# Reading the accumulator banks out in another order in the query, key and value stage of a two-layer attention block

## Chip, cores and metric

One core of one Trainium2 chip runs the whole program in one launch. The metric is the device time of one execution in microseconds (us); the kernel before is given by the median of three runs. All points in time below are microseconds from the start of the profiled execution's span.

## The reference, cut to what matters

Two layers run one after the other on four batches of 512 tokens with 512 features. The change sits at the entry of the second layer's self-attention:

```python
x = rms_norm(hidden_states, ln_in_w)
mixed = jnp.where(vm, x @ v_qkv, x @ l_qkv)
q, k, v = jnp.split(mixed, 3, axis=-1)
q, k, v = (heads(q, NH, HD), heads(k, NH, HD), heads(v, NH, HD))
q, k = apply_rotary(q, k, position_ids, l)
```

`vm` marks the tokens that take the second expert's weights (`v_qkv`); all others take the first's (`l_qkv`). The norm's factor is one number per token, so the kernel multiplies it in behind the products: into the rotary tables for queries and keys, and as a column of factors for the values.

## The kernel before, in words

The stage is the function `queries_values_keys` (from line 687). Each product is made in three matmuls of rounded and rest parts (`three`, lines 103 to 107), so every weight and every token tile is split into a rounded tile and a rest. A batch has three projections of eight steps each: queries, values, keys (in the last batch queries, keys, values). The first four steps of a projection use the first expert, the other four the second; if the flag of early tokens is not set, the second half is narrowed to the last 128 tokens. TensorE reads that flag and branches behind the fourth query step of every batch. The three projections alternate between two groups of four accumulator banks, so a projection starts when the group has been read out.

The order on each engine is written out by hand, and the engines meet only at semaphores:

- TensorE (lines 1074 to 1128): `project` makes one step, `sums` multiplies the summed squares with a matrix of ones (line 1101; two products, the plain norm and the weighted one, into the first two banks of the values' group), and in the fifth value step four small products turn the norm factors into a column (line 1117).
- ScalarE (lines 807 to 906): `round_x` and `round_w` round token and weight tiles (819, 811), `square` squares the stream (829), `keep_plain` copies queries or keys out of the banks (839), `round_piece` rounds a finished piece (846), `root` makes a reciprocal square root by Ln and Exp (859, 861), and `keep_values` reads the values out with the column of factors (871). `root(i, 0)` reads the first sums from their bank; `root(i, 1)` reads what VectorE made of the second.
- VectorE: `mask_x` and `rest_x` prepare tokens (979, 986), `rest_w` makes a weight's rest (967), `second_sums` squares the first root and multiplies it with the second sums out of their bank (994, 997), `tables` makes the factors and the scaled cosine and sine (1003 to 1006), `turn_pieces` does the rotary part of four pieces (1017 to 1027), and then the column is copied out of its bank (1053, tile `rs_col`).
- GpSimd: `add_squares` (919) and `scale_pieces` (930), the cosine products.
- SP issues all loads and stores of the stage: weights (91), the next batch's stream (772), two stores for each finished piece (753, 755) and one for each value tile (792). In the last batch it also loads self-attention's first keys before the last four pieces' stores, and at the end a row of ones (795).

The semaphore `s_tab` counts the five VectorE instructions of the tables; the values' group of banks is free when its second one (the read of the second sums) has run. Weights of the keys are steps 16 to 23: in the first batch ScalarE rounds them behind the copies of the queries, and VectorE makes their rests before it turns the first piece.

Of the kernel before, what the change touches and what calls it, by code (L numbers as in the profile page):

```python
# [7 lines left out]
P = 128  # L8
# [16 lines left out]
def program(nc, t, out):  # L25
# [21 lines left out]
    with ExitStack() as keep:  # L47
# [639 lines left out]
        def queries_values_keys(more_h, more_l, k_r, q_r, v_r, s_key, s_value, s_first):  # L687

            names = ("s_tt s_k s_ku0 s_ku1 s_eu s_hin s_x s_xh s_xl s_sq s_sum s_ss s_rs s_tab s_r0u s_pl s_sf s_t1 s_t2 s_rp s_rh s_rl "
# [13 lines left out]
            with ctx:  # L703
# [27 lines left out]
                with nc.Block() as block:  # L731
                    @block.sync
                    def _(sp):
# [28 lines left out]
                        for i in range(B):  # L762
# [15 lines left out]
                            if i == B - 1:  # L778
# [9 lines left out]
                                for j in range(DT):  # L788
                                    store_piece(2 * DT * i + DT + j)
                            for a in range(ST):  # L790
# [3 lines left out]
                        sp.wait_ge(s["s_wu"], NT * B)  # L794
                        sp.dma_start(k_r[3 * HD:3 * HD + 1, :, :].bitcast(f32).rearrange("a (r h) n -> a r (h n)", r=8),
                                     ones_d[:, 0:SELF_RING * 4 // 8 * S].rearrange("(a r) n -> a r n", a=1)).then_inc(s_first, 16)
# [10 lines left out]
                    def _(act):  # L807
# [40 lines left out]
                        def root(i, n):  # L848
# [10 lines left out]
                            nc.scalar.activation(rs[:, :], src, ACT.Ln, bias=eps_col[:, 0:1], scale=1.0 / D).then_inc(s["s_rs"], 1)  # L859
                            act.wait_ge(s["s_rs"], 4 * i + 2 * n + 1)  # L860
                            nc.scalar.activation(rs[:, :], rs[:, :], ACT.Exp, scale=-0.5).then_inc(s["s_rs"], 1)

                        def keep_values(i):
# [3 lines left out]
                            for a in range(ST):  # L867
                                o = ST * i + a
                                if o >= 2 and not (i == B - 1 and a >= 2):
# [3 lines left out]
                                    .then_inc(s["s_vn"], 1)  # L873

# [7 lines left out]
                        for i in range(B):  # L882
# [9 lines left out]
                            keep_plain(i, 0)  # L892
                            if i == 0:
                                for n in range(2 * G, 3 * G):
                                    round_w(n)
                            for j in range(DT):
# [12 lines left out]
                    def _(pool):  # L909
                        def add_squares(i):  # L910

                            for n in range(2):
                                for k in range(1, DT):
# [3 lines left out]
                                    elif i:  # L917
                                        pool.wait_ge(s["s_ss"], 2 * (i - 1) + n + 1)
                                    nc.gpsimd.tensor_tensor(out=sq[:, 2 + n, :], in0=sq[:, 0 if k == 1 else 2 + n, :], in1=sq[:, k % 2, :],
# [23 lines left out]
                    def _(dve):  # L943
# [45 lines left out]
                        def second_sums(i):  # L989
# [5 lines left out]
                            dve.wait_ge(s["s_ss"], 2 * i + 2)  # L995
                            dve.wait_ge(s["s_tab"], 5 * i + 1)
                            nc.vector.tensor_tensor(out=rs1[:, :], in0=rs1[:, :], in1=ps[:, bank(3 * i + 1, 1), :], op=ALU.mult)\
# [9 lines left out]

                        def turn_pieces(i, group):

                            dve.wait_ge(s["s_tab"], 5 * (i + 1))  # L1010
                            for j in range(DT + 1):
                                o = 2 * DT * i + DT * group + j
                                if j < DT:
# [25 lines left out]
                        for i in range(B):  # L1039
# [10 lines left out]
                            dve.wait_ge(s["s_rc"], i + 1)  # L1050
                            if i:
# [1553 lines left out]
```

## Time and profile before

| | us |
|---|---|
| median of three runs | 2175.74 |
| lowest and highest run | 2171.53, 2179.38 |
| the profiled execution | 2180.68 |
| its span | 2178.7 |
| the stage of the change, in the span | 354.2 to 615.4 |

The profiled execution has a trace of every engine. A timeline row gives the start, the length and the instruction, and in brackets how long its engine stood idle before it and what ended that. Rows of the same line that follow one another are merged (x4), and their lengths may overlap. PE is TensorE, DVE is VectorE, ACT is ScalarE, POOL is GpSimd, SPq is SP's queue of transfers. Of matmuls the starts are recorded and the ends are modelled.

### The profile page before, as it was taken

To read this page: it belongs to the slowest core of one execution; us is meant where nothing else is said; L and a number is where in the kernel's file an instruction comes from. 1 tells how busy PE (TensorE), PEld (TensorE's weight loads), DVE (VectorE), ACT (ScalarE), POOL (GpSimd) and SP (SyncE) were. 2 spreads that over 40 slices of the span, in tenths; PEclk is the share of its full clock that TensorE was granted. 3 is DMA by queue.
4 is the path that set the end of the run, shared out by engine and by line. 5 is a ranking of instruction groups with operands and counts; after the bars stand their busy time and mean duration, and the time that the engine had idled before them with its cause. 6 is when DMAs were issued, how large, how long until landed. Compare 5 with 4: busy or idle time off the path is not lost. (4 is left out here: it accounts for less than half of the span.)

```text
span 2178.7 us, 32799 instructions
## 1 busy us (share of the span) xinstructions
PE 1996.9 (92%) x12654; PEld 1340.6 (62%) x12654; DVE 1523.9 (70%) x2111; ACT 1007.2 (46%) x1748; POOL 509.4 (23%) x496
## 2 busy tenths in 40 slices
PE   6999997799979997788879999999998799999997
PEld 5788875677845554676634444444434677878885
DVE  5676776588847775656579999999952565766563
ACT  1232314455425554444348888888884222221111
POOL 0321231133401222332201312223222212221211
PEclk9999998799969999999979999999999899999998
DMA  3222112333377663685545344354401333334332
GB/s 139 71 99 80 35 57 78 121 122 122 101 189 175 169 151 103 205 254 201 154 114 96 68 89 87 73 98 78 91 14 40 112 92 99 102 109 114 94 97 56
DMA packets 174793, 236.92 MB, mean 109 GB/s; under 512 B 26218, under 2 KB 103022, under 8 KB 172426
## 3 DMA queue, kind: packets, MB, share of 16 engines
q1 hardware_dynamic: 166480, 223.65, 38.3%
q0 software_dynamic: 7856, 10.90, 1.8%
q8 instruction: 112, 1.84, 0.4%
q14 instruction: 57, 0.47, 0.1%
q10 hardware_dynamic: 288, 0.08, 0.0%
HBM read 169.54 MB, written 62.91 MB: 107 GB/s over the span
## 5 line engine op out<-in xcount | busy, mean ns | idle before, releaser
L2120 ACT ACTIVATE pT_x<-ps 128x512 f32<-128x512 f32 (+1 forms) x832 | 451.3, 595 | 84.6 <-PE ps L2218 57.0
L2159 DVE TENSOR_REDUCE quarters<-ps 128x2 f32<-128x804 f32 x480 | 454.1, 992 | 45.5 <-PE ps L2190 44.7
L2233 PE MATMUL ps<-pT_x,vx_ring 128*17 128x256 f32 (+1 forms) x3328 | 261.5, 387 | 0.2 <-ACT osb_x L2102 0.2
L105 PE MATMUL ps<-mi_h,w_hi 128*128 128x512 f32 (+1 forms) x440 | 174.0, 395 | 12.8 <-DVE mi_l L2414 12.8
L2379 POOL TENSOR_TENSOR sg<-sg,keep_all 128x512 f32<-128x512 f32 (+1 forms) x55 | 88.1, 1602 | 386.0 <-ACT sg L2358 386.0
L106 PE MATMUL ps<-mi_h,w_lo 128*128 128x512 f32 (+1 forms) x440 | 173.2, 394 | 0.0
L107 PE MATMUL ps<-mi_l,w_hi 128*128 128x512 f32 (+1 forms) x440 | 173.1, 393 | 0.0
L1307 DVE TENSOR_REDUCE row_max_s<-ps 128x1 f32<-128x384 f32 (+3 forms) x176 | 109.4, 633 | 68.6 <-PE ps L1339 67.8
L1279 ACT ACTIVATE pT_s<-ps 128x512 f32<-128x512 f32 (+1 forms) x176 | 96.0, 558 | 117.6 <-PE ps L1364 115.6
L99 DVE CAST w_hi<-w_raw 128x512 fp32r<-128x512 f32 (+1 forms) x165 | 84.3, 511 | 72.4 <-PE ps L107 65.4
L2233 PEld LDWEIGHTS ps<-pT_x,vx_ring 128*17 128x17 f32 (+1 forms) x3328 | 55.6, 95 | 110.7 <-issue 68.8
L101 DVE TENSOR_TENSOR w_lo<-w_raw,w_hi 128x512 fp32r<-128x512 f32 (+1 forms) x165 | 114.8, 696 | 5.7
L2362 ACT ACTIVATE hid_h<-prod 128x512 fp32r<-128x512 f32 (+1 forms) x55 | 34.8, 634 | 177.4 <-DVE prod L2442 177.4
L2358 ACT ACTIVATE sg<-ps 128x512 f32<-128x512 f32 (+1 forms) x55 | 32.8, 596 | 164.7 <-PE ps L107 164.7
L289 ACT ACTIVATE pT<-ps 128x512 f32<-128x512 f32 (+1 forms) x52 | 31.0, 598 | 158.2 <-PE ps L107 158.2
L105 PEld LDWEIGHTS ps<-mi_h,w_hi 128*128 128x128 f32 (+1 forms) x440 | 82.3, 187 | 33.0 <-issue 13.6
L107 PEld LDWEIGHTS ps<-mi_l,w_hi 128*128 128x128 f32 (+1 forms) x440 | 82.2, 187 | 20.0
L106 PEld LDWEIGHTS ps<-mi_h,w_lo 128*128 128x128 f32 (+1 forms) x440 | 82.3, 187 | 19.1
L2442 DVE TENSOR_TENSOR prod<-ps,sg 128x512 f32<-128x512 f32 (+1 forms) x55 | 37.9, 689 | 80.1 <-PE ps L107 71.3
L105 PE MATMUL ps<-hid_h,w_hi 128*128 128x512 f32 (+1 forms) x220 | 87.9, 400 | 3.0 <-DVE hid_l L2446 3.0
L1339 PE MATMUL ps<-qkv_h,qkv_l 96*128 96x128 f32 (+3 forms) x256 | 90.5, 414 | 0.0
L329 POOL TENSOR_TENSOR sin_t<-sin_t,pT 128x512 f32<-128x512 f32 (+1 forms) x48 | 72.4, 1509 | 65.0 <-ACT pT L289 64.4
(350 smaller groups left out, 4821.0 us busy)
## 6 DMA issues: line engine op xcount, KB each, us to landing
qkv_l<-self_q_by_part SPq DMA_DIRECT2D x48, 256.0 KB, 4.4
qkv_h<-self_k_by_part SPq DMA_DIRECT2D x48, 256.0 KB, 6.7
w_raw<-L_xattn_l_gate SPq DMA_DIRECT2D x40, 256.0 KB, 2.9
w_raw<-L_xattn_l_up SPq DMA_DIRECT2D x40, 256.0 KB, 2.9
w_raw<-L_xattn_l_down SPq DMA_DIRECT2D x40, 256.0 KB, 2.7
kx_first<-cross_k_by_part SPq DMA_DIRECT2D x36, 200.2 KB, 7.2
cross_v_by_group<-v_aug SPq DMA_DIRECT2D x16, 442.0 KB, 3.9
vx_ring<-cross_v_by_group SPq DMA_DIRECT2D x16, 442.0 KB, 10.1
```

Of the source, the lines that this page charges most:

```text
L99: nc.vector.tensor_copy(hi, raw).then_inc(s_high, 1)
L101: nc.vector.tensor_tensor(out=lo, in0=raw, in1=hi.bitcast(f32), op=ALU.subtract).then_inc(s_split, 1)
L105: nc.tensor.matmul(dst, ah, bh, start=start, stop=False, **how)
L106: nc.tensor.matmul(dst, al, bh, start=False, stop=False, **how)
L107: return nc.tensor.matmul(dst, ah, bl, start=False, stop=stop, **how)
L1279: nc.scalar.activation(pT[:, u % 3, j:j + n, 0:width], heads_of(ps[:, SCORES + v % 3, :], n, width), ACT.Exp, scale=SCALE).then_inc(s["s_e ...
L1307: nc.vector.tensor_reduce(out=row_max[:, g % 2, j:j + heads, q], in_=heads_of(bank, heads, (q + 1) * P), axis=AX.X, op=ALU.max)\
L1339: last = nc.tensor.matmul(bank[:, m * width:(m + 1) * width], q_r[0:STACK, at + m, cut], k_r[0:STACK, at + m, 0:width], start=False, stop= ...
L2120: nc.scalar.activation(pT[0:kn, u % 3, j, :], ps[0:kn, 5 + v % 3, :], ACT.Exp, scale=SCALE)\
L2159: nc.vector.tensor_reduce(out=quarters[:, g % 2, pair, :, q, quarter], in_=ps[:, at:at + 2, 0:MAXW], axis=AX.X, op=ALU.max)\
L2233: last = nc.tensor.matmul(ps[j * HD:j * HD + CHD + 1, 4, queries], v_r[0:kn, g % RING, kt, j, :], pT[0:kn, u % 3, j, queries], start=kt == ...
L2379: nc.gpsimd.tensor_tensor(out=by_batch(sg[0:cn, c % 2, :]), in0=by_batch(sg[0:cn, c % 2, :]), in1=keep_all[0:cn, experts[i], :, rows(i)], ...
```

## The change

- The second sums are copied by ScalarE from their bank into the fourth tile of `sq`, between the Ln and the Exp of the first root; VectorE multiplies with that tile. The values' first product waits for this copy (`s_cp`) instead of VectorE's product. GpSimd's next use of the tile waits for VectorE's.
- The column of norm factors is copied before the fourth query piece instead of behind it; in the last batch before the third key piece.
- In the first batch the key weights are rounded before the queries are copied out, and the sums are multiplied behind the sixth query step, so behind the branch, instead of the fourth.
- In the last batch ScalarE issues the four value stores itself, and the row of ones is issued before the last key piece's stores.

```diff
--- before.py
+++ after.py
@@ -686,7 +686,7 @@
 
         def queries_values_keys(more_h, more_l, k_r, q_r, v_r, s_key, s_value, s_first):
 
-            names = ("s_tt s_k s_ku0 s_ku1 s_eu s_hin s_x s_xh s_xl s_sq s_sum s_ss s_rs s_tab s_r0u s_pl s_sf s_t1 s_t2 s_rp s_rh s_rl "
+            names = ("s_tt s_k s_ku0 s_ku1 s_eu s_hin s_x s_xh s_xl s_sq s_sum s_ss s_rs s_tab s_r0u s_cp s_pl s_sf s_t1 s_t2 s_rp s_rh s_rl "
                      "s_uh0 s_uh1 s_ul0 s_ul1 s_ul2 s_rc s_rcc s_vn s_uv0 s_uv1 s_hup " + WSEMS)
             ctx, sems = stage(names)
             s = dict(zip(names.split(), sems))
@@ -785,15 +785,16 @@
                                 self_key_loads(sp, 0, k_r, q_r, s_key)
                                 self_value_load(sp, 0, v_r, s_value)
                                 sp.dma_start(early_d.rearrange("b o n -> o (b n)"), early_v[:, :]).then_inc(s["s_eu"], 16)
-                                for j in range(DT):
+                                for j in range(DT - 1):
                                     store_piece(2 * DT * i + DT + j)
-                            for a in range(ST):
+                                sp.wait_ge(s["s_wu"], NT * B)
+                                sp.dma_start(k_r[3 * HD:3 * HD + 1, :, :].bitcast(f32).rearrange("a (r h) n -> a r (h n)", r=8),
+                                             ones_d[:, 0:SELF_RING * 4 // 8 * S].rearrange("(a r) n -> a r n", a=1)).then_inc(s_first, 16)
+                                store_piece(2 * DT * i + 2 * DT - 1)
+                            for a in range(ST if i < B - 1 else 0):
                                 sp.wait_ge(s["s_vn"], ST * i + a + 1)
                                 sp.dma_start(vs_d[turns[i]].rearrange("g p a n -> p a g n")[:, a, :, :],
                                              value_tile(i, a).rearrange("p (g n) -> p g n", n=P)).then_inc(s_uv[a % 2], 16)
-                        sp.wait_ge(s["s_wu"], NT * B)
-                        sp.dma_start(k_r[3 * HD:3 * HD + 1, :, :].bitcast(f32).rearrange("a (r h) n -> a r (h n)", r=8),
-                                     ones_d[:, 0:SELF_RING * 4 // 8 * S].rearrange("(a r) n -> a r n", a=1)).then_inc(s_first, 16)
                         sp.wait_ge(s["s_eu"], 16)
                         sp.wait_ge(s["s_r0u"], 16 * B)
                         for m in range(2):
@@ -857,6 +858,9 @@
                             else:
                                 act.wait_ge(s["s_tab"], 5 * i + 2)
                             nc.scalar.activation(rs[:, :], src, ACT.Ln, bias=eps_col[:, 0:1], scale=1.0 / D).then_inc(s["s_rs"], 1)
+                            if n == 0:
+                                act.wait_ge(s["s_ss"], 2 * i + 2)
+                                nc.scalar.activation(sq[:, 3, :], ps[:, bank(3 * i + 1, 1), :], ACT.Copy).then_inc(s["s_cp"], 1)
                             act.wait_ge(s["s_rs"], 4 * i + 2 * n + 1)
                             nc.scalar.activation(rs[:, :], rs[:, :], ACT.Exp, scale=-0.5).then_inc(s["s_rs"], 1)
 
@@ -871,6 +875,10 @@
                                 nc.scalar.activation(value_tile(i, a), ps[:, bank(3 * i + place(i, 1), a), :], ACT.Copy,
                                                      scale=rs_col[:, a:a + 1])\
                                     .then_inc(s["s_vn"], 1)
+                                if i == B - 1:
+                                    act.wait_ge(s["s_vn"], o + 1)
+                                    act.dma_start(vs_d[turns[i]].rearrange("g p a n -> p a g n")[:, a, :, :],
+                                                  value_tile(i, a).rearrange("p (g n) -> p g n", n=P)).then_inc(s_uv[a % 2], 16)
 
                         for n in range(2 * DT):
                             round_x(0, n)
@@ -889,10 +897,10 @@
                                 for j in range(2, DT):
                                     round_piece(2 * DT * (i - 1) + DT + j)
                             root(i, 1)
-                            keep_plain(i, 0)
                             if i == 0:
                                 for n in range(2 * G, 3 * G):
                                     round_w(n)
+                            keep_plain(i, 0)
                             for j in range(DT):
                                 round_piece(2 * DT * i + j)
                             if i == B - 1:
@@ -916,6 +924,8 @@
                                         pool.wait_ge(s["s_sum"], 3 * (2 * i + n) + k - 1)
                                     elif i:
                                         pool.wait_ge(s["s_ss"], 2 * (i - 1) + n + 1)
+                                        if n:
+                                            pool.wait_ge(s["s_tab"], 5 * (i - 1) + 2)
                                     nc.gpsimd.tensor_tensor(out=sq[:, 2 + n, :], in0=sq[:, 0 if k == 1 else 2 + n, :], in1=sq[:, k % 2, :],
                                                             op=ALU.add).then_inc(s["s_sum"], 1)
 
@@ -992,9 +1002,9 @@
                             if i:
                                 dve.wait_ge(s["s_rc"], i)
                             nc.vector.tensor_tensor(out=rs1[:, :], in0=rs0[:, :], in1=rs0[:, :], op=ALU.mult).then_inc(s["s_tab"], 1)
-                            dve.wait_ge(s["s_ss"], 2 * i + 2)
+                            dve.wait_ge(s["s_cp"], i + 1)
                             dve.wait_ge(s["s_tab"], 5 * i + 1)
-                            nc.vector.tensor_tensor(out=rs1[:, :], in0=rs1[:, :], in1=ps[:, bank(3 * i + 1, 1), :], op=ALU.mult)\
+                            nc.vector.tensor_tensor(out=rs1[:, :], in0=rs1[:, :], in1=sq[:, 3, :], op=ALU.mult)\
                                 .then_inc(s["s_tab"], 1)
 
                         def tables(i):
@@ -1005,11 +1015,20 @@
                             nc.vector.tensor_tensor(out=cos_r[:, :], in0=cos_t[:, :], in1=rs1[:, :], op=ALU.mult).then_inc(s["s_tab"], 1)
                             nc.vector.tensor_tensor(out=sin_r[:, :], in0=sin_t[:, :], in1=rs1[:, :], op=ALU.mult).then_inc(s["s_tab"], 1)
 
+                        def keep_columns(i):
+
+                            dve.wait_ge(s["s_rc"], i + 1)
+                            if i:
+                                dve.wait_ge(s["s_vn"], ST * i)
+                            nc.vector.tensor_copy(rs_col[:, :], ps[:, bank(3 * i + place(i, 1) - 1, 0), 0:ST]).then_inc(s["s_rcc"], 1)
+
                         def turn_pieces(i, group):
 
                             dve.wait_ge(s["s_tab"], 5 * (i + 1))
                             for j in range(DT + 1):
                                 o = 2 * DT * i + DT * group + j
+                                if (j, group) == ((DT - 1, 0) if i < B - 1 else (2, 1)):
+                                    keep_columns(i)
                                 if j < DT:
                                     dve.wait_ge(s["s_pl"], o + 1)
                                     if o:
@@ -1047,10 +1066,6 @@
                             turn_pieces(i, 0)
                             if i == B - 1:
                                 turn_pieces(i, 1)
-                            dve.wait_ge(s["s_rc"], i + 1)
-                            if i:
-                                dve.wait_ge(s["s_vn"], ST * i)
-                            nc.vector.tensor_copy(rs_col[:, :], ps[:, bank(3 * i + place(i, 1) - 1, 0), 0:ST]).then_inc(s["s_rcc"], 1)
                             if i + 1 < B:
                                 find_keep(i + 1)
                                 for n in range(2 * DT + 1):
@@ -1074,7 +1089,7 @@
                                     if i:
                                         pe.wait_ge(s["s_vn"], ST * i)
                                 elif place(i, part) == 1:
-                                    pe.wait_ge(s["s_tab"], 5 * i + 2)
+                                    pe.wait_ge(s["s_cp"], i + 1)
                                     if i:
                                         pe.wait_ge(s["s_pl"], 2 * DT * i)
                                 else:
@@ -1107,7 +1122,7 @@
                             for m in steps:
                                 n = G * parts[m // G] + m % G
                                 project(i, n, t0)
-                                if m == 3:
+                                if m == (3 if i else 5):
                                     sums(i, 0)
                                     sums(i, 1)
                                 if n == G + 4:
```

## Rows read from the trace of the kernel before

**Rows 1.** Busy time in a stretch (TensorE matmul, TensorE load, VectorE, ScalarE, GpSimd), then granted clock.

```profile
423.40:479.70 56.30, 52.97 (x264) 43.94 (x265) 46.05 (x69) 28.76 (x45) 21.53 (x14) 0.94 0.34 118
```

**Rows 2.** Waits of TensorE, 345 to 625 us: us in total, times, longest.

```profile
PE ps L105 <- DVE rs_col L1053: 10.0, 3, 7.4
...
PE ps L105 <- DVE rs L997: 6.8, 3, 2.8
PE ps L1101 <- POOL sq L919: 6.3, 2, 4.0
...
PE ps L105 <- issue: 3.8, 1, 3.8
```

**Rows 3.** Timeline of TensorE, first batch: start, us, instruction, idle before it.

```profile
381.92 2.08 PE L1101 MATMUL ps<-sq,ones 128*128 128x512 f32 x2 [3.97 <-POOL sq L919]
387.75 0.45 PE L105 MATMUL ps<-xe1h,qkv_h 128*128 128x128 f32 x1 [3.76 <-issue]
```

**Rows 4.** Timeline of ScalarE, first batch.

```profile
382.52 1.28 ACT L861 ACT_TABLE_LOAD   x1
383.82 0.63 ACT L861 ACTIVATE rs<-rs 128x512 f32<-128x512 f32 x1
...
399.51 2.06 ACT L839 ACTIVATE plain<-ps 128x512 f32<-128x512 f32 x4 [10.84 <-PE ps L107]
...
410.02 0.64 ACT L811 ACTIVATE qkv_h<-w_raw 128x512 fp32r<-128x512 f32 x1 [0.95 <-DMA w_raw<-L_xattn_v_qkv]
```

**Rows 5.** Timeline of VectorE, first batch.

```profile
390.03 0.68 DVE L1006 TENSOR_TENSOR sin_r<-sin_t,rs 128x512 f32<-128x512 f32 x1
402.12 4.11 DVE L967 TENSOR_TENSOR qkv_l<-w_raw,qkv_h 128x512 fp32r<-128x512 f32 x4 [11.40 <-ACT qkv_h L811]
...
411.31 0.74 DVE L1017 STREAM_SHUFFLE swapped<-plain 128x512 f32<-128x512 f32 x1
```

**Rows 6.** Timeline of GpSimd, first and second batch.

```profile
400.25 4.23 POOL L930 TENSOR_TENSOR t<-plain,cos_r 128x512 f32<-128x512 f32 x3 [18.38 <-ACT plain L839]
...
465.94 4.70 POOL L930 TENSOR_TENSOR t<-plain,cos_r 128x512 f32<-128x512 f32 x3 [8.96 <-DVE sin_r L1006]
```

**Rows 7.** Timeline of SP's queue, value stores of the first and second batch.

```profile
424.08 1.00 SPq L792 DMA_DIRECT2D self_v_by_group<-v_nat  x2
...
480.38 5.82 SPq L792 DMA_DIRECT2D self_v_by_group<-v_nat  x4
```

**Rows 8.** Timeline of VectorE, second batch: first and fourth query piece, norm columns.

```profile
465.90 0.74 DVE L1017 STREAM_SHUFFLE swapped<-plain 128x512 f32<-128x512 f32 x1
...
475.55 0.76 DVE L1017 STREAM_SHUFFLE swapped<-plain 128x512 f32<-128x512 f32 x1
...
479.43 0.16 DVE L1053 COPY rs_col<-ps 128x4 f32<-128x4 f32 x1
```

**Rows 9.** Timeline of ScalarE, second batch: a token rounding, the third key piece.

```profile
433.54 0.63 ACT L819 ACTIVATE xe0h<-full_x 128x512 fp32r<-128x512 f32 x1 [1.57 <-PE ps L107]
...
456.98 0.61 ACT L846 ACTIVATE rows_h<-t 128x512 fp32r<-128x512 f32 x1
```

**Rows 10.** Timeline of VectorE, second batch: rests of the last two key pieces.

```profile
458.25 1.47 DVE L1027 TENSOR_TENSOR t<-t,rows_h 128x512 fp32r<-128x512 f32 x2
```

**Rows 11.** Timeline of VectorE, last batch: third key piece.

```profile
598.30 0.74 DVE L1017 STREAM_SHUFFLE swapped<-plain 128x512 f32<-128x512 f32 x1
```

**Rows 12.** Timeline of TensorE, norm columns of the second and the last batch.

```profile
474.49 1.05 PE L1117 MATMUL ps<-ones,rs 1*128 1x1 f32 x8
...
602.55 1.05 PE L1117 MATMUL ps<-ones,rs 1*128 1x1 f32 x8
```

**Rows 13.** Timeline of ScalarE, last batch: last key piece.

```profile
605.81 0.63 ACT L846 ACTIVATE rows_h<-t 128x512 fp32r<-128x512 f32 x1 [2.11 <-DVE t L1023]
```

**Rows 14.** Tile ident: ScalarE's issue, ns min/median/max.

```profile
L263 ACTq DMA_DIRECT2D ident<-c_ident x1: 426/426/426, 0.7 to 0.7; - x1
```

**Rows 15.** Timeline of SP's queue, last batch: last value stores.

```profile
609.19 1.49 SPq L792 DMA_DIRECT2D self_v_by_group<-full_x  x2
```

## Prediction

> **What bounds the kernel now.** The change touches one stage, from 354.2 to 615.4 us of the span, so I read that stage and left the page's totals. First the busy times from one start of the key projection to the next [rows 1]: TensorE is busy 52.97 of 56.3 us, VectorE 46.05. That alone would make TensorE the limit. Then who keeps TensorE waiting [rows 2]: the norm-column copy (rs_col, 10.0 us in three waits, the longest 7.4, in the first batch), the second-sum product (rs, 6.8 in three), GpSimd's sums of squares (6.3, both in the first batch), and one gap of 3.8 that no other engine explains. The first two end on the read-out side. So a ring sets the period: ScalarE reads the values out, rounds the next batch's tokens and reads the keys out; VectorE turns the key pieces, makes the tables, turns the query pieces, and its norm-column copy lets the values be read. TensorE's idle time counts only where it delays a link of this ring.
>
> I work against the profiled execution, 2180.68 us (span 2178.7 and 2.0 around it); the median of the three runs is 4.9 us lower, and I take the gain in us off that median. A measurement of this kernel can tell about 0.3%, here 6.5 us.
>
> **First batch: the only large term.** Now TensorE finishes its fourth query step, waits for GpSimd's second sum, multiplies it from 381.92 to 384.00, and stands 3.76 us before the next product [rows 3]; that gap holds the branch on the early flag. After the change two more steps lie in front of the sums, so the branch comes while products are still queued. Every batch has this branch, and the list of waits has a gap of this size once [rows 2]. I take it as covered; if the cover fails it costs up to 3.8 (a rival). GpSimd's sum is not moved, so the second sum product still ends at 384.0 (between 381.9, the wait alone, and 387.8 with the gap).
>
> On ScalarE the first root's Exp ends at 383.82 + 0.63 = 384.45 [rows 4]. The new Copy waits in front of that Exp for the second product: 384.0 + 0.6 (four plain copies take 2.06, about 0.5 each, plus a hand-over), then the Exp's table load, 1.28 [rows 4], then Exp 0.63: 386.6, so 2.15 later. What follows, up to the sine table, keeps its instructions: 390.03 + 0.68 = 390.71 becomes 392.9 [rows 5]. Bounds of a Copy between Ln and Exp: 0 if it slips into waiting time, one more table load (1.28) if it needs its own; the trace has Copy only behind Exp, without a load, so I take none.
>
> Key weights: now VectorE's first split of them starts at 402.12, because ScalarE rounds them behind four copies that wait for the queries, at 399.51 [rows 4, 5]. Between 390.71 and 402.12 VectorE has nothing to do. With the rounding first, the first split follows the sine table at 392.9. From first split to first turned piece the trace takes 411.31 - 402.12 = 9.2 [rows 5]: SP reloads four weight buffers as splits free them, and the last rounding, held by its load, ends at 410.02 + 0.64, that is 8.5 after the first split [rows 4]. The same 9.2 gives 402.1. The price is that the query copies stand behind the last rounding: from 392.9 + 8.5 = 401.4 instead of 399.5, just ahead of VectorE. **So the first turn starts 9.2 us earlier.** If the loads are no faster than half of this, 4.6.
>
> This turn then loses a cover. Today GpSimd's three cosine products run from 400.25, before VectorE begins; in the next batch they start together with it at 465.94 [rows 6]. From first turned piece to first value store it is 424.08 - 411.31 = 12.8 in the first batch and 480.38 - 465.90 = 14.5 in the second [rows 5, 7, 8]. The first batch now behaves as the second: store at 402.1 + 14.5 = 416.6, **7.5 us earlier**; at best, without that stretch, 9.2.
>
> **Norm columns between pieces.** The copy is issued before the fourth piece, in the second batch 475.55 instead of 479.43 [rows 8]. TensorE's keys can start some 4 us sooner. But ScalarE cannot: its fourth rounding still comes first, and SP issues the value stores behind the fourth piece's store, so the first store moves by 0.3 at most, and 0.2 go to the copy itself. I count nothing. What TensorE gives back: in the first token loop ScalarE waits twice for products, 1.57 in the row shown [rows 9]. Such waits go; VectorE is nearly gapless beside them, so I take **0.5** once (0 to 3.1).
>
> **Second sums by ScalarE.** TensorE's values no longer wait for VectorE's product: 6.8 us of TensorE idle [rows 2] go, but off the ring; TensorE then waits for the norm columns instead. The Copy costs ScalarE 0.5 per batch. Behind it stands the third key piece's rounding, 456.98 + 0.61 = 457.6, whose reader on VectorE starts at 458.25 [rows 9, 10]: 0.65 slack, so 0; uncovered it is at most 0.5 x 3 = 1.5.
>
> VectorE's product now reads two SBUF tiles, like the sine multiply (0.68, alone) [rows 5]. At that point GpSimd stands idle until the sine table exists, 8.96 us in the second batch [rows 6]; I add nothing. The Trainium skill (GPSIMD Engine Reference, section 1, Specifications) says the two engines contend for SBUF when a VectorE instruction has two SBUF inputs, which speaks against the move out of PSUM. By that rule alone the 1.7 us stretch above would be the scale of the loss, some 1.7 per batch, where both engines work; here they don't.
>
> **Last batch and tail.** ScalarE stands some 0.2 before the last key copies, for TensorE; that goes, **0.2**. Norm columns before the third key piece: VectorE now reaches that piece at 598.30, and TensorE's columns end at 602.55 + 1.05 = 603.6 [rows 11, 12]. TensorE gains on the ring twice: its keys one batch before start 479.43 - 475.55 = 3.9 sooner [rows 8], and up to 2.8 more go with the wait on rs. So with the ring at -8.2 the columns end near 603.6 - 8.2 - 6.7 = 588.7, against an arrival at 598.3 - 8.2 + 0.2 = 590.3: no wait. The values then follow ScalarE's last rounding (605.81 + 0.63 = 606.4) [rows 13] and no longer for the columns. But ScalarE now issues each store itself: four reads of about 0.65 with the hand-over, and between them three issues of 0.43 (ScalarE's only kind of issue in the trace) to 0.75 (SP's for these tiles) [rows 14, 15], give 3.9 to 4.85 from last rounding to last issue; now the last of SP's two goes at about 609.9, 3.5 behind it. **Loss 0.9** (0.4 to 1.4). The row of ones, moved on SP past the last key piece's store, costs that store one issue; it still lands before the values. In the first batches SP's order is unchanged.
>
> Sum: -7.5 - 0.5 - 0.2 + 0.9 = **-7.3 us**; 2175.74 - 7.3 = **2168.4**. The next stage begins behind a barrier and all of it follows, so the gain passes through.
>
> **Rivals.**
> 1. *The branch gap stays.* The gap of rows 3 follows the branch into the first-batch sums: the ring starts up to 3.8 later, gain 3.5, 2172.2. For: the gap is there with nothing else that the profile names. Against: the other batches show none. The Trainium skill (Runtime: NRT & Kernel Launch, section Instruction fetch mechanics) says that a taken branch breaks the sequential prefetch and stalls; no run here shows whether queued products cover it in this batch. Chance 0.17.
> 2. *The weights come no sooner.* ScalarE's rounding stands on the loads and the query copies stand behind it, so half of the 9.2 goes: -2.7, 2173.0. Chance 0.10.
> 3. *TensorE is the bound after all.* Then all its waits but the first and the seam go: 10.0 + 6.8 + 6.3 + 3.8 = 26.9 [rows 2, 3], 2148.8. For: 94% busy. Against: each of those waits ends on the ring. Chance 0.07.
> 4. *Slower: VectorE blocks on the norm columns.* With its copy between pieces, VectorE stands still if the columns come after it. Today they end at 475.54 when it arrives at 475.55, and in the last batch 5.3 after it [rows 8, 11, 12]. If TensorE's columns fall x behind the ring in the last three batches, the loss is 3x + 5.3; from x = 2.8 it eats the gain and 0.3% more; at 3 it is 14.3 - 7.3 = +7.0, 2182.7. For: the margin today is nil. Against: the wait in front of the values is what the change shortens. Chance 0.06.
>
> **Numbers.** Forecast 0.60. Its own bounds: best, the sums 2.1 sooner and the stretch of 1.7 away, -11.1; worst, an extra table load, the Copy uncovered, the dearer issues and nothing for the token loop, -3.5. About three quarters of it lie beyond 6.5: 0.45, with rival 3 faster 0.52. Same: 0.15 + 0.17 + 0.10 = 0.42. Slower 0.06. The range of 2163.5 to 2174.0 takes in the forecast's bounds and rivals 1 and 2 with a little of the scatter of the three runs; 3 and 4 stay outside.
>
> **What would show it.** Right: first turned piece near 402, its Exp near 386.6, first value store near 416.6, no TensorE wait on rs, but waits on rs_col of some 4 to 5 us left in three batches, periods of the store still 55 to 56, self-attention's first product near 608. Wrong: the gap before the second query half still 3.8 with the sums behind it (rival 1), weight roundings that end after 404 (2), a period near 50 (3), VectorE idle before rs_col (4).

## Result and profile after

The median after is 2161.45 us (2159.43 to 2162.76, five runs) against 2175.74 before: ratio 0.9926, interval 0.9908 to 0.9943. The kernel is 14.3 us faster where 7.3 were forecast, 2 us below the low end of the range. The span fell from 2178.7 to 2159.6; 5.2 of these 19.1 lie behind the stage, where nothing was changed, and the profiled execution before was 4.9 above its median. I therefore measure the stage in the traces: from the first masked token tile to the first product of self-attention it took 258.28 before and 244.85 after, **13.4 us less**.

TensorE's waits from 345 to 625 us, kernel after (us, times, longest), answer to [rows 2]:

```profile
PE ps L105 <- DVE rs_col L1023: 11.4, 3, 4.7
...
PE ps L106 <- issue: 2.5, 1, 2.5
...
PE ps L1116 <- POOL sq L929: 0.8, 1, 0.8
```

The wait on rs is gone and the norm columns have three of 3 to 5 us, much as forecast. The gap behind the branch is still 2.5 us long, but now it lies ahead of the sums (timeline of TensorE, against [rows 3]):

```profile
376.85 0.22 PE L106 MATMUL ps<-xe1h,qkv_l 128*128 128x128 f32 x1 [2.52 <-issue]
...
381.48 2.07 PE L1116 MATMUL ps<-sq,ones 128*128 128x512 f32 x2 [0.81 <-POOL sq L929]
```

ScalarE, first batch (against [rows 4]): Copy, table load, Exp, then the roundings ahead of the query copies.

```profile
383.59 0.60 ACT L863 ACTIVATE sq<-ps 128x512 f32<-128x512 f32 x1 [1.53 <-PE ps L1116]
384.20 1.28 ACT L865 ACT_TABLE_LOAD   x1
385.50 0.63 ACT L865 ACTIVATE rs<-rs 128x512 f32<-128x512 f32 x1
...
398.48 1.28 ACT L812 ACTIVATE qkv_h<-w_raw 128x512 fp32r<-128x512 f32 x2 [1.46 <-DMA w_raw<-L_xattn_v_qkv]
399.66 2.04 ACT L840 ACTIVATE plain<-ps 128x512 f32<-128x512 f32 x4
```

VectorE (against [rows 5]): the first four splits take 2.49 us instead of 4.11, and the first turned piece starts at 400.40 instead of 411.31.

```profile
392.32 2.49 DVE L977 TENSOR_TENSOR qkv_l<-w_raw,qkv_h 128x512 fp32r<-128x512 f32 x4
...
400.40 0.75 DVE L1036 STREAM_SHUFFLE swapped<-plain 128x512 f32<-128x512 f32 x1
...
409.70 0.16 DVE L1023 COPY rs_col<-ps 128x4 f32<-128x4 f32 x1
```

SP's value stores of the first two batches (against [rows 7]): 9.85 and 11.7 us earlier.

```profile
414.23 5.00 SPq L796 DMA_DIRECT2D self_v_by_group<-v_nat  x4
...
468.70 1.17 SPq L796 DMA_DIRECT2D self_v_by_group<-v_nat  x2
```

And one link of the ring that the prediction left as it was: the third value read of a batch waits until the first stored tile has landed, and the fourth until the second has. ScalarE's list of waits before had it (345 to 625 us; us in total, times, longest):

```profile
ACT v_nat L871 <- DMA self_v_by_group<-v_nat: 10.7, 3, 3.6
```

ScalarE before, then after:

```profile
423.36 1.26 ACT L871 ACTIVATE v_nat<-ps,rs_col 128x512 f32<-128x512 f32 x2 [0.89 <-DVE rs_col L1053]
428.27 1.39 ACT L871 ACTIVATE v_nat<-ps,rs_col 128x512 f32<-128x512 f32 x2 [3.64 <-DMA self_v_by_group<-v_nat]
```

```profile
412.84 1.25 ACT L875 ACTIVATE v_nat<-ps,rs_col 128x512 f32<-128x512 f32 x2
417.27 0.69 ACT L875 ACTIVATE v_nat<-ps,rs_col 128x512 f32<-128x512 f32 x1 [3.18 <-DMA self_v_by_group<-v_nat]
418.17 0.69 ACT L875 ACTIVATE v_nat<-ps,rs_col 128x512 f32<-128x512 f32 x1 [0.21 <-DMA self_v_by_group<-v_nat]
```

I call the time from the store's issue to the third read the landing: it is 4.19 us before (4.04 and 4.12 in the next batches) and 3.04 after (3.08, 2.84). SP also issues the store a little nearer behind the last piece's store, 0.80 us before and 0.49 after (SP's queue, last piece's store before, then after); counted from that store the third read comes at 4.99 and 3.53.

```profile
423.28 0.45 SPq L755 DMA_DIRECT2D self_q_by_part<-t  x1
```

```profile
413.74 0.45 SPq L755 DMA_DIRECT2D self_q_by_part<-t  x1
```

The transfer view of before, 424 to 428 us in 40 slices (DMA share in tenths, GB/s), shows what the late microsecond is:

```profile
DMA  9999998998899889899898989898999840000000
GB/s 348 369 492 369 369 389 308 348 410 307 348 430 389 267 231 256 200 297 333 261 302 266 277 251 312 261 302 282 302 287 292 256 113 26 20 26 20 20 21 20
...
q8 instruction: 1, 0.02, 1.9%
```

From 427.3 on some 20 GB/s are left of about 300, a sixteenth, so one engine's worth; and in the window lies one packet of instructions (queue q8, 0.02 MB), whose 1.9% of 16 engines over 4 us are 1.2 us of one engine. I take q8 for TensorE's queue, because its packets move when TensorE's code alone is changed (below). The packet comes 1.5 us after TensorE's first key product, which the norm-column copy sets free. After the change the copy is 4.5 us ahead of the store, and the packet, some 2 us behind the copy, is ahead of it too: the view of 410 to 414 us has it, that of 414 to 418 has none.

```profile
q8 instruction: 1, 0.02, 1.4%
```

### The profile page after: what moved, and what is told of

It is laid out like the page before. It is cut to its first block and busy times, and to the rows that moved or that the text cites. A ratio compares the mean times of both kernels' runs of the same rounds, so it can differ in the third digit from the quotient of the medians.

```text
span 2159.6 us, 32786 instructions
## 1 busy us (share of the span) xinstructions
PE 1990.5 (92%) x12637; PEld 1335.5 (62%) x12654; DVE 1520.9 (70%) x2111; ACT 1009.4 (47%) x1752; POOL 510.8 (24%) x496
## 5 line engine op out<-in xcount | busy, mean ns | idle before, releaser
L106 PEld LDWEIGHTS ps<-mi_h,w_lo 128*128 128x128 f32 (+1 forms) x440 | 82.0, 186 | 19.1
```

Of the source, the lines that this page charges most:

```text
L106: nc.tensor.matmul(dst, al, bh, start=False, stop=False, **how)
```

## Experiments

All times below marked "from t0" count from the first masked token tile, so that later stages and the start don't enter; "stage" is the whole from t0 to self-attention's first product. Periods are from value store to value store. A ratio is to the kernel before, measured along with that run, so medians of different runs are not to be subtracted. Each run has one trace. The part behind the stage, which no run changes, takes 1555.6 to 1563.3 us in them, so I compare stages; and equal work in front of a change starts up to 1 us apart (first key split before and in the runs of norm columns, last stores and packet: 43.96 to 44.98 from t0), so a difference in the stage below 1 us says little. The code cuts are condensed.

**First-batch edits alone.**

```diff
-keep_plain(i, 0); if i == 0: round_w(2G..3G)
+if i == 0: round_w(2G..3G); keep_plain(i, 0)
-if m == 3: sums
+if m == (3 if i else 5): sums
```

> The kernel before with the first-batch part alone (key weights rounded first, sums behind the sixth query step). Reload account (the predicted -7.5 was too small by 1.1 for the reload chain, which runs faster without GpSimd beside it): first turned piece 8.1 us behind the first split of the key weights instead of 9.2, first value store near 414.5, the stage shorter by 9 to 10, and the periods from value store to value store unchanged at 55.8 to 56.3, the third value read still 4.0 to 4.2 behind the first store. Rival (the whole gain is one chain that this part starts): the later periods are 54.4 here too and the stage is shorter by 12 to 13.

Measured 2163.11, ratio 0.9938 (0.9915 to 0.9961). First turned piece 41.49 from t0 (54.17 before, 43.73 with the whole change), first store 55.61 (66.94, 57.56), stage 246.05: 12.2 of the 13.4 us. The edits of the first batch carry nearly all of the gain, and without ScalarE's Copy they start the ring 2.2 us sooner still. The stage is the rival's (12 to 13), the periods are the first account's (56.65 and 55.99, not 54.4): the first account had its first store near 414.5, as in the whole change, with the Copy's delay in it; it came at 410.9. The landing is 4.08 and 4.12 with the packet in the store's window, and in the third batch, where the packet missed it, 3.08.

**Norm columns between pieces alone** (only `keep_columns` moved).

> The kernel before with the norm columns copied between pieces, nothing else. Fetch account (a block of TensorE's instructions is fetched when it begins the keys, and while the value stores run it holds one of their 16 DMA engines about 1.0 longer; begun earlier it misses them): third value read 3.0 to 3.2 behind the first store, no instruction packet between, each of the first three periods shorter by 1.2 to 1.4. In the last batch VectorE then meets the columns late and stands 1 to 5, so the stage is between 3 shorter and 1 longer. Account of the prediction (worth nothing in the first batches): periods unchanged, stage 1 to 5 longer through the last batch.

Measured 2177.3, ratio 1.0002 (0.9992 to 1.0012). The landing falls to 3.04, 3.08, 3.26 and the first two periods from 56.3 and 55.8 to 55.32 and 55.0; the last batch gives it back. VectorE, last batch of this kernel:

```profile
600.74 0.16 DVE L1013 COPY rs_col<-ps 128x4 f32<-128x4 f32 x1 [5.27 <-PE ps L1122]
```

This is the place of rival 4 and the wait that it named (5.3): alone, this edit does block VectorE.

**Second sums by ScalarE alone** (Copy, and its readers and waits).

> The kernel before with the second sums copied by ScalarE, nothing else. Prediction (off the ring): TensorE's wait on rs goes, 6.8 in three, its wait on rs_col grows by as much, stage within 1 of before, less 0.5 for the token loop, plus 2.1 in the first batch where the Exp comes later but the weights bound it anyway, so -0.5 to +0.5. Rival (TensorE begins the keys sooner and with it the fetch): -2 to -4.

Measured 2178.45, ratio 0.9999 (0.999 to 1.0009). Stage 258.86, first turned piece 54.0: alone it gains nothing.

**Last stores by ScalarE and the row of ones alone.**

> The kernel before with the last value stores on ScalarE's queue and the row of ones issued earlier, nothing else. Prediction: 0.4 to 1.4 longer. What the changed kernel's trace suggests (9.21 instead of 8.94 from last rounding to the next stage): 0.3 longer, with 0.9 less if the columns' wait stays in it, so -0.5 to +1.0 in the stage and nothing that the times can tell.

Measured 2177.65, ratio 1.0 (0.999 to 1.001). From the last rounding to self-attention's first product 9.29 us (8.98 before): a cost of 0.3, not 0.9.

**Keys kept back, in the kernel after.** TensorE's keys wait as before for the end of the query pieces, VectorE's copy stays early.

```diff
 pe.wait_ge(s["s_rcc"], i + 1)
+if i < B - 1:
+    pe.wait_ge(s["s_rl"], 2 * DT * i + DT)
```

> The changed kernel, but in the first three batches TensorE's keys also wait for the rest of the fourth query piece, so they begin where they began before the change; the column copy, ScalarE's reads and SP's order stay as changed. Fetch account: the instruction block falls into the value stores again, the third value read comes 4.0 to 4.2 behind the first store where a packet is seen and 3.1 where not, each such period about 1.0 longer, the token loop meets its products late once (0.5): stage 2.5 to 4 longer, 247.4 to 249. Queue account (the stores land sooner because SP issues them right behind the piece's stores with both tiles already read): third read stays at 3.0 to 3.1, stage less than 0.7 longer.

Measured 2168.93, ratio 0.9957 (0.994 to 0.9974); stage 252.82, 8.0 more than after, where 2.5 to 4 were expected. The landing is 4.46 and 4.42 again, with the packet in the window, and 3.27 in the third batch, without. At the fourth value read, where the token roundings begin, the first two make 2.4 of the 8.0. Much of the rest is TensorE's lateness: ScalarE's token roundings, which waited for no product in the kernel after, now wait for seven microseconds (waits of ScalarE, 410 to 530 us), and VectorE stands 2.1 us for the norm columns of the last batch:

```profile
ACT xe0h L820 <- PE ps L107: 7.1, 5, 1.6
```

So the earlier keys are worth more than the landing, and this run alone cannot say whether the packet or the earlier keys shorten it. The next does.

**The packet moved, in the kernel before.** The four norm-column products are issued three times in a row, which writes the same columns; TensorE's code grows by eight products per batch.

```diff
-for a in range(ST):
+for a in 3 * list(range(ST)):
     last = nc.tensor.matmul(
```

> The kernel before, with TensorE's four norm-column products issued three times in a row (the same columns are written again), 8 products more a batch and nothing else. Times are counted from the first masked token tile. Before: the trace has one packet of TensorE's instructions 1.4 us after each norm-column copy, 0.8 us after the first value store is issued, and the third value read starts 4.0 to 4.2 us after that store. Theory (the packet holds one DMA engine and the store ends when the slowest part lands): the longer code crosses its block boundary ahead of the copy, the packet leaves the store's window in the three batches, the third read follows the store by 3.0 to 3.3 us, the two periods shorten by some 1.0 each, the stage from 258.3 to 255 to 256, the time by 2 to 3.5 us, though TensorE does more. Rival (the store lands sooner because TensorE's keys start sooner, or because of something else that the early copy moves): the third read stays at 4.0 to 4.2, the stage 258 to 260 with the extra products.

Measured 2183.16, ratio 1.0033 (1.0018 to 1.0048). The landing did what the packet theory says, and more: the third read follows the store by 2.73, 2.39 and 2.35 us. The first batch is the clean case: the copy, and the keys behind it, are as late as before (0.97 us ahead of the store, before 0.96), and SP issues the store 0.80 us behind the last piece's store, as before. Counted from that store the third read comes at 3.53, as in the kernel after, against 4.99 before. (In the later batches the copy is some 2 us ahead, because TensorE's late values delay the reads.) SP and ScalarE, and the transfers of 420 to 424 us:

```profile
419.31 0.44 SPq L755 DMA_DIRECT2D self_q_by_part<-t  x1
420.11 4.73 SPq L792 DMA_DIRECT2D self_v_by_group<-v_nat  x4
```

```profile
422.84 0.69 ACT L871 ACTIVATE v_nat<-ps,rs_col 128x512 f32<-128x512 f32 x1 [2.18 <-DMA self_v_by_group<-v_nat]
```

```profile
GB/s 308 369 389 389 430 410 348 348 205 348 389 389 389 353 256 251 246 256 343 323 302 276 292 267 297 282 297 282 292 287 297 287 175 16 0 0 0 0 0 0
...
q1 hardware_dynamic: 1348, 1.04, 79.5%
```

No packet, and no tail like the one before, with about as many bytes as before (1.04 MB, before 1.02 and the packet). The time, though, went the other way: the stage is 265.96 where 255 to 256 were expected. The extra products take 2.83 us where the four took 1.05, and TensorE, late by that much, becomes what ScalarE waits for (11.2 us in the token loops, 5.1 before; and VectorE stands 4.4 us for a query copy). The expectation gave the extra products no price; TensorE's waits were not spare.

**Rounding not first, in the kernel after** (`keep_plain` ahead of the roundings again).

> The changed kernel with the key weights rounded behind the query copies again. The prediction's step (rounding first is what brings the weights forward): first split back at 402 less what the queries gain, first turn some 8 to 10 later than in the changed kernel, stage 253 to 255. Rival (the sums behind the sixth step already end the queries near 389, so the copies stand in front of the rounding for some 2 us only): first split 1.5 to 2.5 later, stage 246 to 247.5.

Measured 2167.08, ratio 0.9949 (0.9932 to 0.9966). First split 35.45 from t0, the same (the rival had it 1.5 to 2.5 later); first turned piece 45.37 instead of 43.73, stage 245.96. Rounding first is worth 1.1 to 1.6, not the nine that I gave it: with the sums behind the sixth step the queries are ready when the roots are, and their copies hold ScalarE for 2.0 us only. What is lost lies behind the first split: GpSimd's products, which need those copies, stand beside the splits again, five splits take 6.08 us, and SP's four reloads 4.5 (after: 2.49 for four splits, 2.3). VectorE, then GpSimd:

```profile
392.09 6.08 DVE L977 TENSOR_TENSOR qkv_l<-w_raw,qkv_h 128x512 fp32r<-128x512 f32 x5 [0.45 <-ACT qkv_h L812]
```

```profile
391.72 4.70 POOL L940 TENSOR_TENSOR t<-plain,cos_r 128x512 f32<-128x512 f32 x3 [10.33 <-DVE sin_r L1016]
```

**Sums at the fourth step, in the kernel after.**

> The kernel after, with the sums of squares of the first batch behind TensorE's fourth step again instead of the sixth; key weights are still rounded ahead of the query copies. Theory (each of the two first-batch edits frees the weights by itself: rounding first does not wait for queries, early queries do not hold rounding): first split 35 to 36 and first turned piece 43.5 to 45 (after: 35.65 and 43.73; with the sums moved and the rounding not: 35.45 and 45.37), stage 244.5 to 246. Rival (the gap of 3.8 us in TensorE before its second query half comes back and holds the ring): first turned piece 46 to 48, stage 247 to 249.

Measured 2165.4, ratio 0.9958 (0.9943 to 0.9974). First split 35.63 and first turned piece 43.02: with the rounding first, the weights come early whatever TensorE does. But the first store is 3.2 later and the stage 247.85, the rival's figure, by another way than it had: TensorE's wait for GpSimd's second sum (3.97 us, after 0.81) and its gaps are back, and the norm columns come too late for the new place of their copy. TensorE, then VectorE:

```profile
384.02 0.44 PE L105 MATMUL ps<-xe1h,qkv_h 128*128 128x128 f32 x1 [3.04 <-issue]
387.22 0.27 PE L106 MATMUL ps<-xe1h,qkv_l 128*128 128x128 f32 x1 [1.48 <-issue]
```

```profile
410.56 0.16 DVE L1023 COPY rs_col<-ps 128x4 f32<-128x4 f32 x1 [4.04 <-PE ps L1132]
```

**Second sums not by ScalarE, in the kernel after.**

> The changed kernel with VectorE reading the second sums out of their bank again. The prediction's step (in the first batch the Copy and its wait hold the Exp 2.15 back, later it is hidden): first turn 2 us sooner, near 41.5 behind the first token tile, and the stage 1.7 to 2.2 shorter, 242.6 to 243.2. Rival (the Copy is what lets the values begin in time, so without it the norm columns come late for VectorE in some batch): first turn sooner, but 1 to 4 lost in the later periods, stage 244 to 247.

Measured 2162.73, ratio 0.9934 (0.991 to 0.9959); stage 248.31. The ring starts 2.2 us sooner, and VectorE then stands 1.20, 0.97 and 5.27 us for norm columns. In the whole change the Copy pays for the column part; alone it pays for nothing.

**Third and fourth value tile in other memory, in the kernel after**, so that no value read waits for a store (the waits that go with the tiles are moved too).

```diff
-return full[:, a - 2, :] if i == B - 1 and a >= 2 else v_nat[:, a % 2, :]
+return v_nat[:, a, :] if a < 2 else (full if i == B - 1 else plain)[:, a - 2, :]
```

> The changed kernel, with the third and fourth value tile of the first three batches in the first two tiles of plain, which are free then, so that ScalarE's reads wait for no store. If the store's landing is a link of the ring, as both accounts say: ScalarE's first token rounding then waits for VectorE's masked tile instead, about 2 us sooner per batch, periods 52.3 to 52.6, stage 5 to 7 shorter, 238 to 240. If the ring is held elsewhere (VectorE's own work): less than 1 shorter.

Measured 2157.71, ratio 0.9908 (0.9892 to 0.9925); stage 240.4, 4.5 less than after, a little under the expected 5 to 7: the landing was on the ring even at 3.0.

**No Copy in the first batch, in the kernel after** (VectorE and TensorE wait there as before the change), and then **both together**, with the tiles.

```diff
-if n == 0:
+if n == 0 and i:
     act.wait_ge(s["s_ss"], 2 * i + 2)
```

> The kernel after, with the ScalarE Copy of the second sums from the second batch on alone; in the first, VectorE's product reads the bank itself and TensorE's values wait for that product, as before. Theory (the Copy stands in front of the first batch's Exp and costs it the wait and a place, 2.1 us, on the ring): first split of the key weights 33.5 and first turned piece 41.5 after the first masked token tile (35.65 and 43.73 in the kernel after), periods unchanged, stage 242.7 (244.85), time 2.1 us below the kernel after. Rival (TensorE's columns come too late again, as where the second sums were not on ScalarE at all): the two start times move, but VectorE waits 1 to 5 us for norm columns in later batches and the stage stays at 244.5 to 247.

> Both at once: the Copy from the second batch on alone, and the third and fourth value tile of the first three batches in the tile that held the plain pieces, so that no value read waits for a store. Theory (both lie on the ring and add): stage 240.4 - 2.1 = 238.3, time about 2155.6. Rival (with the ring this short TensorE is the limit, or norm columns are late): stage 240 to 241 as with the tiles alone, 2157.7.

Measured 2158.93, ratio 0.993 (0.9916 to 0.9944), and 2155.71, ratio 0.9909 (0.9895 to 0.9923). The first: first turned piece 41.48, stage 243.39, and VectorE waits for norm columns once, 0.3 us; 1.5 of the 2.1 arrive. The second: stage 236.31, 8.5 below the kernel after, the lowest of all and 2 below the expected 238.3. The times do not tell it from the tiles alone (ratio 0.9908), and its interval overlaps that of the kernel after. Its second period (busy times by engine, as in [rows 1]) has TensorE at 98% (94% before, by the same count):

```profile
411.00:464.00 53.00, 51.77 (x273) 43.27 (x273) 45.95 (x69) 29.01 (x46) 21.32 (x14) 0.99 0.36 125
```

## Why the prediction fell short

The direction and the largest term were right; one step that was counted as nothing was not nothing, and two sizes were off. By the prediction's own steps, in the stage (the last column counts a landing where it reaches the token roundings, at the fourth value read):

| step | forecast | measured | what it was |
|---|---|---|---|
| first value store | -7.5 | -9.4 | splits and reloads quicker, turn less stretched |
| first to second store | -0.5 | -1.8 | landing -0.96, token loop -0.56, store nearer behind the pieces -0.31 |
| second to third store | 0 | -1.4 | landing -0.83, from the last key turn to the tables -0.4 |
| third store to last rounding | -0.2 | -1.1 | landing -0.68, last query pieces -0.83, losses of 0.4 |
| tail | +0.9 | +0.3 | the row of ones no longer ends it (not tried) |
| sum | -7.3 | -13.4 | |

**The step that failed is "Norm columns between pieces ... I count nothing".** It asked when the value store is issued and found that it moves by 0.3 at most; it did not ask when the store lands, though two of four value reads hang on that. The landing shortened by 3.4 us over three batches; 2.5 of it reaches the token roundings, because the fourth read still waits for the second store. That is the largest part of the 6.1 us that the forecast misses in the stage. The keys moved on TensorE drag their instruction packet with them, out of the store's window. In the twelve traces in which the read waits, the 13 batches with the packet in the window had the third read at 4.0 to 4.5 us and the 23 without at 2.4 to 3.3, in the same kernel too (first-batch edits alone, keys kept back), and moving the packet in the kernel before took the late microsecond away.

**Mis-sized: the first batch.** The first split came where forecast (35.65 from t0; forecast 392.9, which is 35.8). "The same 9.2" from there to the first turned piece was 8.1: without GpSimd's products beside them four splits take 2.49 us instead of 4.11, buffers come free sooner, and SP issues the four reloads in 2.3 us instead of 3.4. [Rows 5, 6] held this: the 4.11 stood beside GpSimd's 4.23; and with the rounding put back the splits are slow again beside GpSimd's products and it is 9.9 to the first turned piece. From turn to store it was 13.8, between the two batches that I had to choose from. Those two give the 1.9.

**Mis-sized: the tail.** The last value store is issued 4.2 us behind the last rounding, within the forecast's 3.9 to 4.85. But I took SP's last value store for the end of the tail before; behind it SP still issued the row of ones (first row), which the change has moved ahead. That this is the missing 0.6 is read from the order, not tried. SP's queue before, then ScalarE's after:

```profile
610.72 0.83 SPq L795 DMA_DIRECT2D qkv_h<-ones_rows  x1
```

```profile
596.47 0.50 ACTq L880 DMA_DIRECT2D self_v_by_group<-full_x  x1
```

**Misattributed: rounding first.** I gave the 9.2 to the rounding's place. Either edit of the first batch alone frees the weights; the second of them adds 1.1 (rounding first) or 3.0 (sums behind the sixth step), as the two runs that undo one show.

**Right:** the Copy in front of the Exp (2.15 forecast; without it the first split comes 2.1 and the first turned piece 2.2 sooner); the token loop (0.5; 0.56); TensorE's waits on rs gone and on rs_col left; the second sums off the ring (alone, nothing); the key weights ended long before 404. The forecast periods of 55 to 56 were wrong (54.47 and 54.44), and self-attention's first product came at 601.5, not near 608.

**Rivals.** 1: the gap exists (3.0 when the sums go back) and is covered here; with the sums back the stage is 3.0 longer, through the norm columns, but TensorE's longer wait for GpSimd's second sum is in that too, and the gap's own share was not tried. A q8 packet starts inside the gap before (384.82 us), after (374.42) and with the sums back (381.33). The Trainium skill (Runtime: NRT & Kernel Launch, section Instruction fetch mechanics) says that a taken branch stalls for a fetch by DMA when its target is not in the pages at hand; the trace agrees in the gap of 2.5 that remains and the packet in it, and shows that this gap costs nothing ahead of a wait. 2: no, the weights came when forecast. 3: not here (periods of 54.5, TensorE still waits for the norm columns); with both extra edits it comes near (53.0 and 52.4). 4: real where the Copy or the later sums are missing (5.27 and 4.04), smaller with the keys kept back or the rounding not first (2.12, 1.23), practically absent in the whole (0.15), as its "against" said.

**Not settled:** with repeated columns the landing of the first batch is shorter (2.73) than after (3.04) only because the store is issued later behind the last piece's store; counted from that one both are 3.53. In its later batches the store stands 1.8 to 2.1 us behind the piece's, which may explain 2.4; this was not tried. What part of the last batch's 0.83 is whose stays open too, and so does the row of ones.

## What to carry to other kernels

Where a reader waits for a store, cost the store to its landing, and look at what else the transfer engines carry in that window, instruction packets included. Price the parts of a change together as well as alone: here one part alone gains 12.2 of 13.4 us, three gain nothing alone, and two of the parts (the Copy and the later sums) are needed to keep the early column copy from blocking VectorE. The idle time of an engine is spare only up to the point where its next product is read.

## What was not expected of the hardware

- One packet of TensorE's instructions (0.02 MB, 0.9 to 1.2 us of one of 16 transfer engines by the two rows above) delays the landing of a 256 KB store under way by about as much: 1.0 to 1.5 us, counted from the last piece's store (4.99 before against 3.53 with the packet moved; 4.9 against 3.87 among the batches of the first-batch edits alone).
- Adding eight small products to TensorE shortened a store's landing by 1.5 us (4.19 to 2.73): TensorE's instruction packet no longer fell into it.
- TensorE's gap of 2.5 us behind the branch cost nothing ahead of a wait. VectorE beside GpSimd did cost: four splits took 2.49 us alone, 4.11 with GpSimd's products beside part of them, and five took 6.08 with GpSimd beside most of them.
